# A mixture of experts on one core: seven of eight batches computed for the two picked experts only, on sorted blocks

## The reference

```python
def _mla(h, ...):      # causal attention, 16 heads of 8
    ...
def _moe(h, gate_w, w1, w2):             # 8 experts, 2 picked
    t = h.reshape(B * S, D)
    logits = t @ gate_w
    top_v, top_i = jax.lax.top_k(logits, 2)
    gates = jax.nn.softmax(top_v, axis=-1)
    combine = zeros((T, 8)).at[arange(T)[:, None], top_i].add(gates)
    hid = silu(einsum('td,edh->teh', t, w1))     # w1: 8 x 128 x 256
    ye = einsum('teh,ehd->ted', hid, w2)         # w2: 8 x 256 x 128
    return einsum('te,ted->td', combine, ye)
x = x + _mla(_rmsnorm(x, g1), ...)
x = x + _moe(_rmsnorm(x, g2), gate_w, w1, w2)
return _layernorm(x)
```

## Time and profile before

| | us |
|---|---|
| median of three runs | 658.04 (655.24 to 666.04) |
| span of the profiled execution | 658.2 |
| TensorE busy | 629.6 (96%) |
| VectorE busy | 511.7 (78%) |
| ScalarE busy | 426.6 (65%) |
| GpSimd busy | 250.2 (38%) |

### The profile page before, as it was taken

One profiled execution on the slowest core, in us unless ns is written; L12 is line 12 of the kernel. 1 busy time (PEld: TensorE's weight loads), 2 busy tenths in 40 slices (PEclk: granted clock), 3 DMA queues, 4 the chain that ended last, 5 costly groups with the idle time before them and its releaser, 6 DMA issues.

```text
span 658.2 us, 14254 instructions
## 1 busy us (share of the span) xinstructions
PE 629.6 (96%) x5056; PEld 420.7 (64%) x5056; DVE 511.7 (78%) x1871; ACT 426.6 (65%) x779; POOL 250.2 (38%) x317
## 2 busy tenths in 40 slices
PE   8999889888999999999999999999999999999996
PEld 4586545454556767676766666767676766666885
DVE  4756968958688899878888788878887888873676
ACT  4663456666667677867686768676867676756443
POOL 8130322222323365335334533353334333543442
PEclk9999968998899999999999999999999999999998
DMA  8700000000000000000000000000000000000000
GB/s 313 213 19 17 0 1 1 1 2 0 1 1 2 2 1 1 18 1 1 2 17 1 1 2 17 2 0 2 17 1 2 1 17 1 2 1 17 1 18 17
DMA packets 10072, 12.17 MB, mean 18 GB/s; under 512 B 1609, under 2 KB 8210, under 8 KB 9746
## 3 DMA queue, kind: packets, MB, share of 16 engines
q1 hardware_dynamic: 9250, 11.25, 5.2%
q10 hardware_dynamic: 752, 0.01, 0.1%
HBM read 9.16 MB, written 2.10 MB: 17 GB/s over the span
## 4 chain that ended last, share of the span: by engine, by line
PE 73%; DVE 9%; ACT 4%; issue 2%; POOL 1%; DVEq 0%; ACTq 0%; POOLq 0%
PE turn L1043 16%; PE turn L1035 14%; PE psV L1093 11%; PE psW L1081 10%; PE turn L997 6%; PE turn L987 3%; PE psS L1064 3%; DVE psS L1310 3%; PE turn L1005 2%; ACT prob L1218 1%; PE turn L1027 1%; PE turn L1016 1%; PE turn L936 1%; PE turn L928 1%; ACT X L1112 1%
## 5 line engine op out<-in xcount | busy, mean ns | idle before, releaser
L1218 ACT ACTIVATE prob<-psW 128x1024 f32<-128x1024 f32 (+1 forms) x192 | 183.1, 954 | 103.3 <-PE psW L1081 102.7
L1310 DVE CUSTOM_DVE_ANT_0 psS<-psS,maskb 128x512 f32<-128x512 f32 (+2 forms) x498 | 232.3, 518 | 19.3 <-PE psS L1064 18.4
L894 POOL TENSOR_SCALAR_AFFINE_SELECT prob<-prob 128x512 f32<-128x512 f32 x128 | 80.0, 636 | 223.4 <-ACT prob L1218 223.4
L1043 PE MATMUL turn<-wexp,late 128*128 128x128 f32 x1016 | 126.5, 278 | 0.4 <-DVE late L1370 0.4
L1043 PEld LDWEIGHTS turn<-wexp,late 128*128 128x128 f32 x1016 | 118.9, 192 | 5.7 <-issue 3.6
L1370 DVE SCALAR_TENSOR_TENSOR late<-late,turn 128x512 f32<-128x512 f32 x128 | 87.5, 685 | 37.5 <-ACT late L1180 37.0
L1180 ACT ACTIVATE late<-turn 128x512 f32<-128x512 f32 x128 | 76.3, 597 | 47.9 <-PE turn L1035 38.9
L905 POOL TENSOR_TENSOR late<-late 128x512 f32<-128x512 f32 x62 | 80.0, 1290 | 52.5 <-DVE late L1399 47.3
L1081 PE MATMUL psW<-qT,kT 26*128 26x256 f32 (+2 forms) x512 | 94.0, 404 | 4.5 <-ACT prob L1218 4.0
L1064 PE MATMUL psS<-kT,qT 24*128 24x256 f32 (+1 forms) x498 | 91.7, 405 | 2.0 <-DVE top L1310 1.7
L1093 PE MATMUL psV<-prob,va 128*32 128x512 f32 (+3 forms) x1024 | 90.7, 449 | 0.0
(11 more groups left out here) (273 smaller groups left out, 874.6 us busy)
## 6 DMA issues: line engine op xcount, KB each, us to landing
prob<-in_xT SPq DMA_DIRECT2D x4, 512.0 KB, 6.5
X<-in_x SPq DMA_DIRECT2D x1, 2048.0 KB, 15.8
out<-late SPq DMA_DIRECT2D x8, 256.0 KB, 2.3
prob<-in_wqkvT SPq DMA_DIRECT2D x1, 1024.0 KB
late<-in_w SPq DMA_DIRECT2D x1, 1024.0 KB, 10.7
prob<-in_wqkvT SPq DMA_DIRECT2D x2, 256.0 KB, 3.5
late<-in_woutT SPq DMA_DIRECT2D x1, 512.0 KB
oT<-base_rows SPq DMA_DIRECT2D x2, 256.0 KB, 3.8
```

The source lines that it names most:

```text
L894: pool.affine_select(out=blk, in_=blk, compare_op=ALU.is_ge, fill=0.0, base=0, pattern=[[0, 4], [1, P]], channel_multiplier=-1).then_inc(s ...
L1043: last = mm(into[:, D * c:D * c + D], hid[:, n % 2, k, P * c:P * c + P], wexp2[:, n, k, :], start=(k == 0), stop=(k == 1))
L1218: A(into, src, ACT.Exp).then_inc(s["exp_ready"], 1)
L1310: last = V.tensor_tensor_reduce(at, at, maskb[:, T - P * (c + 1):T], 1.0, BIG, ALU.add, ALU.max, top[:, u % 2, c, 2 * p + j:2 * p + j + 1])
```

## The change

Batch 7 (DENSE) keeps all experts for all tokens, but its up unit is one fp32 matmul of 512 columns. Batches 0 to 6 form the groups (0, 1), (2, 3), (4, 5) and (6). In a group each token has two picked experts, and each pick gets a row of a table in DRAM, sorted by expert, every expert's rows starting on a multiple of 128. The number of blocks of 128 rows is fixed at the most that can occur: 23 for two batches, 15 for one. In order of the steps:

- count and slots: TensorE counts the picks (bf16), VectorE makes from it each pick's row (index) and each block's expert (block_of), 17 small operations.
- spread: GpSimd scatters the tokens by an indirect transfer of 128 rows of 512 bytes, one for each 128 tokens and pick: 16 for two batches, 8 for batch 6, 56 in all.
- for each unit of 4 blocks, SyncE loads a block's expert number into a register and issues two transfers of 128 KB for its w1 and w2 from DRAM into a ring of 8 (weights in), then one that fetches the unit's rows, up to 256 KB (fetch). TensorE transposes them (turned), ScalarE copies them to SBUF (tokens), TensorE multiplies two blocks into a bank (pair), ScalarE takes tanh, VectorE gates, TensorE multiplies down (blocks down), ScalarE copies (save), SyncE stores (store).
- collect: GpSimd gathers each token's two results, again 56 indirect transfers; mix: VectorE adds them, weighted by gates, to the residual, which now stands in X.

The scaling of the weights (g2, 0.5) in the first layer goes, and the split of w1 too; it moves to ScalarE's copy of the tokens and into the shares. At the start of the second part SyncE clears both sorted tables, 3 MB. UNREAD_AT is not changed.

```diff
+GROUPS = [(0, 1), (2, 3), (4, 5), (6,)]
+DENSE = B - 1
+BLOCKS = [2 * n + NE - 1 for n in CHUNKS]
+UNIT = 4
+W_RING = 8
...
-UNITS = {"usual": (13, 1.0, 3), 6: (13, 1.0, 3), 7: (14.5, 1.0, 4)}
+UNITS = (14.5, 1.0, 4)
...
+BLOCKS_FROM = {0: (73.0, 1.9), 1: (121.0, 1.9), 2: (169.0, 1.0), 3: (195.0, 0.7)}
+COUNT_AT, SLOTS_AT, GATES_AT = 38.2, 38.4, 41.0
+SPREAD_FROM, SPREAD_PITCH = 38.7, 0.45
+COLLECT_AFTER, COLLECT_PITCH = 2.0, 0.45
+AFTER_COLLECT = {"mix": 1.5, "norm": 1.9, "norm root": 2.3, "result": 3.3}
...
+def group_steps(put):
+    for g, batches in enumerate(GROUPS):
+        ended = SLOTS * batches[-1]
+        begin, pitch = BLOCKS_FROM[g]
+        units = GROUP_UNITS[g]
+        put(ended + COUNT_AT, "count", g, 0)
+        put(ended + SLOTS_AT, "slots", g, 0)
+        put(ended + GATES_AT, "gates", g, 0)
+        for j in range(2 * CHUNKS[g]):
+            put(ended + SPREAD_FROM + SPREAD_PITCH * j, "spread", g, j)
+        for u in range(units):
+            load = begin - 3.0 + 0.5 * u if u < 2 else begin + pitch * (4 * u - 4.85)
+            put(load, "weights in", g, u)
+            put(load + 0.01, "fetch", g, u)
+            turn = begin - 1.0 if u == 0 else begin + pitch * (4 * u - 2)
+            put(turn, "turned", g, u)
...
+            for v in range(2):
+                at = begin + pitch * (4 * u + v)
+                put(at, "pair", g, 2 * u + v)
...
+            down = begin + pitch * (4 * u + 3)
+            put(down, "blocks down", g, u)
+            put(down + 0.6, "save", g, u)
+            put(down + 0.65, "store", g, u)
+        at = begin + pitch * (4 * units - 1) + COLLECT_AFTER
+        for b in batches:
+            for j in range(2 * C):
+                put(at + COLLECT_PITCH * j, "collect", b, j)
...
         def _(sp):
+            for what, b, n in order:
+                if what == "weights in":
+                    if n == 0:
+                        sp.wait_ge(s["owners_ready"], b + 1)
+                    q = units_before[b] + n
+                    if q >= 2:
+                        wait_full(sp, "blocks down", *unit_at[q - 2])
+                    for i in range(UNIT * n, UNIT * n + in_unit(b, n)):
...
+                        e = sp.value_load(block_of[0:1, b, i:i + 1], min_val=0, max_val=NE - 1)
+                        sp.dma_start(ring_w1(j), keep["w1_of"][ds(e, 1), :, :].rearrange("o p h -> (o p) h")
+                                     ).then_inc(ring_in[j % W_RING], 16)
+                        sp.dma_start(ring_w2(j), keep["w2_of"][ds(e, 1), :, :].rearrange("o p h -> (o p) h")
+                                     ).then_inc(ring_in[j % W_RING], 16)
+                elif what == "fetch":
+                    sp.wait_ge(s["spread_in"], 16 * moves_before[b + 1])
...
         def _(pool):
+                elif what == "spread":
...
+                    pool.indirect_dma_start(keep["sorted"][b % 2], bass.IndirectOffsetOnAxis(index[:, b, k, j:j + 1], 0),
+                                            t[:, k, :], None).then_inc(s["spread_in"], 16)
+                elif what == "collect":
...
+                        wait(pool, "mixed", b)
+                    pool.indirect_dma_start(back[:, c, j, :], None, keep["results"][g % 2],
+                                            bass.IndirectOffsetOnAxis(index[:, g, k, j:j + 1], 0)
+                                            ).then_inc(s["collected"], 16)
...
         def _(pe):
                 elif what == "hidden":
-                    for i, (w, v) in enumerate(((w1h, tTh), (w1h, tTl), (w1l, tTh))):
-                        last = mm(into[:, :], w[:, e, P * k:P * k + P], v[:, :], start=(i == 0), stop=(i == 2))
+                    mm(into[:, :], w1[:, e, P * k:P * k + P], tT[:, :], start=True,
+                       stop=True).then_inc(is_full(*step), 1)
+                elif what == "turned":
+                    q = units_before[b] + n
+                    pe.wait_ge(came_in[q % 2], 16 * (q // 2 + 1))
+                    for k in range(in_unit(b, n)):
+                        last = tr(into[:, P * k:P * k + P], came[:, q % 2, k, :], ident[:, :])
+                elif what == "pair":
...
+                    for i in range(in_pair(b, n)):
+                        j = blocks_before[b] + 2 * n + i
+                        pe.wait_ge(ring_in[j % W_RING], 32 * (j // W_RING + 1))
+                        for k in range(2):
+                            at = P * (2 * i + k)
+                            last = mm(into[:, at:at + P], ring_w1(j)[:, P * k:P * k + P],
+                                      sortedT[:, q % 2, P * (2 * v + i):P * (2 * v + i) + P], start=True, stop=True)
...
         def _(dve):
+                elif what == "mix":
+                    g = GROUP_OF[b]
+                    dve.wait_ge(s["collected"], 16 * 2 * C * (b + 1))
+                    dve.wait_ge(s["both_ready"], b + 1)
...
+                            last = V.scalar_tensor_tensor(out=X[:, C * b + c, :], in0=back[:, c, j, :],
+                                                          scalar=gates[:, g, k, j:j + 1], in1=X[:, C * b + c, :],
+                                                          op0=ALU.mult, op1=ALU.add)
```

More of the change, by code:

```diff
@@ L665 @@
 ROWS_FROM, ROWS_PITCH = -11.5, 1.5
-IN_TURN = ("rest", "apply", "half parts", "half scores", "half outputs", "half delta", "turn", "attnT", "project", "tokensT", "logits", "again", "keys", "queries", "nextT", "qkv", "hidden",
+BLOCKS_FROM = {0: (73.0, 1.9), 1: (121.0, 1.9), 2: (169.0, 1.0), 3: (195.0, 0.7)}
[3 more added lines that the diff above has]
+AFTER_COLLECT = {"mix": 1.5, "norm": 1.9, "norm root": 2.3, "result": 3.3}
+IN_TURN = ("rest", "count", "turned", "pair", "blocks down", "apply", "half parts", "half scores", "half outputs", "half delta", "turn", "attnT", "project", "tokensT", "logits", "again", "keys", "queries", "nextT", "qkv", "hidden",
            "down")
@@ L677, in expert_units @@
     return units
+def group_steps(put):
[14 more added lines that the diff above has]
+            put(turn, "turned", g, u)
+            put(turn + 0.3, "tokens", g, u)
+            for v in range(2):
+                at = begin + pitch * (4 * u + v)
+                put(at, "pair", g, 2 * u + v)
+                put(at + 0.35, "pair tanh", g, 2 * u + v)
+                put(at + 0.75, "pair gate", g, 2 * u + v)
+            down = begin + pitch * (4 * u + 3)
[6 more added lines that the diff above has]
+                put(at + COLLECT_PITCH * j, "collect", b, j)
+            at += COLLECT_PITCH * 2 * C
+            for what, later in AFTER_COLLECT.items():
+                put(at + later, what, b, 0)
+            at += AFTER_COLLECT["mix"]
 def steps_in_order():
@@ L701, in steps_in_order @@
                 put(first + WEIGHT_STEPS * g + at, what, b, g)
-        begin, pitch, lead = UNITS.get(b, UNITS["usual"])
-        for i, (what, n) in enumerate(expert_units(lead)):
+        begin, pitch, lead = UNITS
+        for i, (what, n) in enumerate(expert_units(lead) if b == DENSE else []):
             slot = first + SLOTS + begin + pitch * i
@@ L712, in steps_in_order @@
                     put(slot + pitch * IN_SLOT["unit"], "rest", b, n)
-        for (what, n), at in OF_BATCH.items():
-            own = OF_LAST if b == B - 1 else OF_SECOND if b == 1 else {}
-            put(first + own.get((what, n), at), what, b, n)
+        own = OF_LAST if b == B - 1 else OF_SECOND if b == 1 else {}
+        for (what, n), at in (OF_BATCH | own).items():
+            put(first + at, what, b, n)
         if b >= ROWS_EARLY:
@@ L823, in wait, with used_by, hid_of, t_chunks @@
                 eng.wait_ge(s[name], count)
+        units_before = [sum(GROUP_UNITS[:g]) for g in range(len(GROUPS) + 1)]
+        blocks_before = [sum(BLOCKS[:g]) for g in range(len(GROUPS) + 1)]
+        moves_before = [2 * sum(CHUNKS[:g]) for g in range(len(GROUPS) + 1)]
+        unit_at = [(g, u) for g, n in enumerate(GROUP_UNITS) for u in range(n)]
+        hidden_at = [step for step in order if step[0] in ("pair", "hidden")]
+        hidden_no = {step: i for i, step in enumerate(hidden_at)}
+        def used_by(i):
+            what, at, n = hidden_at[i]
+            return ("blocks down", at, n // 2) if what == "pair" else ("down", at, n // 2)
+        def hid_of(b, n, k):
+            return hid[:, hidden_no[("hidden", b, 2 * n + k)] % 4, :]
+        def t_chunks(b):
+            first = C * GROUPS[GROUP_OF[b]].index(b) if b in GROUP_OF else 0
+            return slice(first, first + C)
+        def in_unit(g, u):
+            return min(UNIT, BLOCKS[g] - UNIT * u)
+        def in_pair(g, v):
+            return min(2, BLOCKS[g] - 2 * v)
+        def ring_w1(j):
+            k = j % W_RING
+            return prob[:, 2, k, 0:EH] if k < 4 else ring[:, k - 4, 0:EH]
+        def ring_w2(j):
+            k = j % W_RING
+            return prob[:, 3, k, 0:EH] if k < 4 else ring[:, k - 4, EH:2 * EH]
```

(4 more changed lines are left out.)

319 lines of the change are left out of this document (243 added, 76 removed).

## The result

| | before | after |
|---|---|---|
| median | 658.96 us (655.24 to 666.04) | 792.43 us (785.58 to 796.7) |
| profiled execution, span | 658.2 us | 786.5 us |
| mean granted clock | 0.98 | 0.83 |

The ratio is 1.201, 95% interval 1.191 to 1.212: slower by a fifth, where 644 us (600 to 688) was predicted; it is taken from undisturbed runs alone, so it is not quite the quotient of the two medians. The change missed its forecast by 148 us, and in the wrong direction.

What follows compares the result with a forecast made beforehand. TensorE was taken to bound the kernel. Head 85.5, slots 0-37 99.9, 37-73 86, 73-169 226, then (57.6 + 12), tail (53.6 + 13 + 2.7) and 8 for group starts gave 644 us, range 600 to 688.

Steps and rivals of the forecast that it cites:

- counting and mixing: VectorE, slots 73 to 169: some 44 small operations for slots and gates, 11 us, and 32 mixing operations, 9.1 us.
- indirect moves: GpSimd: 56 scatters and 56 gathers at 1.04 us each, said to be covered at that price, not at 1.65.
- floor of a slot: Slots 73 to 169: three engines near 2 us plus 0.3 to 0.4 for waits, 2.35 a slot, 226 us (202 to 261).
- The block: TensorE: one transpose, two up and two down fp32 matmuls, 1.0 us a block, 84 us in all.
- Slots 37 to 73: Stage without expert work for batches 0 and 1: 2.4 us a slot, 86 us (76 to 104).
- 94 us leave TensorE: TensorE: 178 us of dense work in seven batches becomes 84 us of sorted blocks, so 94 us leave.
- C: Rival on queues: a scatter at 1.65 us or a SyncE block above 2.5 us adds 30 to 45, 680 us; chance 0.12.
- D: Rival: VectorE and ScalarE hold 2.6 us a slot, adding 24 us, 668 us; chance 0.11.
- SyncE: SyncE's queue: a register load of 0.6 us and two issues of 0.43, 1.5 us a block (0.9 to 3.1).
- Group starts: Where a group follows another, the fetch stands behind four loads: 4 us twice, 8 us in all.
- rival B: Clock falls to 0.50 in slots 37 to 73 and a third of 73 to 169: 696 us; chance 0.14.
- Batch 7 in plain fp32: Tail: an up unit as one fp32 matmul of 512 columns takes 0.87 us against 0.70, 2.7 us more.

Runs made afterwards that it cites:

- kernel with blocks only: The changed kernel without scatters, gathers and weight loads, its sorted blocks reading resident weights and zeroed rows; counting and mixing stay: 721.8 us.
- bare blocks: The changed kernel with its 84 blocks on resident weights and zeroed rows, without count, slot work, gate shares, scatters, gathers or mixes: 651.3 us; in rounds 653.3, ratio 0.990.
- attention only: The changed kernel without any sorted-expert work for batches 0 to 6; attention, norm, store and batch 7's dense experts stay: 592.4 us.
- with fillers: The changed kernel without sorted-expert work for batches 0 to 6, plus one to three unread 128x512 matmuls a slot from slot 45 to 230: 609.2 us.
- filling the whole kernel: The whole changed kernel with 227 more unread 128x512 matmuls in slots 45 to 230, one or two a slot: 812.5 us.
- placed kernel: The whole changed kernel with scatters and gathers later and further apart, and mixes and the blocks of all groups later: 763.5 us.
- count and slots only: Blocks on resident weights and zeroed rows, no moves or mixes, against the changed kernel; count, slot work, gate shares and GpSimd's slot wait kept: 689.0 us.

## Why the prediction was wrong, step by step

From slot 37 on the prediction's sum has 459 us, and the kernel took 600.7. By the table above the 142 us between them are 40 in the blocks beside the attention (30 in slots 73 to 169, 10 behind them), 60 in counting and mixing, 10 in the weight loads beyond the 33 that were priced, and 31 in the indirect moves. So three steps failed: the floor of a slot, the price of counting and mixing by busy time, and the indirect moves, which were put at nothing.

**The block: right.** 1.0 us a block on TensorE was predicted. In the kernel with blocks only the up matmuls of a pair of blocks take 0.90 us by starts at full clock (428.12 to 429.02), 0.45 a block as priced, and the bare blocks add 57 us of time for 84. Slots 37 to 73 were put at 86 us; the bare kernel has 85.7, the changed one, with its first count and scatters in them, 97.3.

**The floor of a slot: 30 us too low.** The prediction had three engines near 2 us a slot in slots 73 to 169 and added 0.3 to 0.4 for their order: 2.35, 226 us. The attention with nothing else runs at 2.28 there (218.7), so the waits between engines already made the slot, and a block is for the most part work on that chain and not in a gap: bare, 2.67 a slot, 256.3 us. The 2.1 was read from seven slots and taken for all: attention only, slots 73 to 85 do run at 2.04, but 85 to 97 at 2.46 and 109 to 121 at 2.48 (at full clock, with fillers, 2.16, 2.39 and 2.31). "94 us leave TensorE" stands and was no gain: most of the 178 us of dense matmuls had stood in slack, and all of them were worth 69 us.

**Counting and mixing: priced by busy time, about 60 us missed.** The step "some 44 small ones for slots and gates, 11 us" and "32 mixing operations, 9.1 us" put them into VectorE's sum (and 32 mixes into a stage that by the places of the change holds 16). They are chains that stand ahead of maxima on VectorE, and GpSimd, ScalarE and TensorE wait at the head of their queues for their results. This is the term that failed most. No rival held it: C had queues, but for the length of an issue, and D had VectorE's load, 24 us.

**SyncE: right in kind, size close.** 1.5 us a block, measured 1.57. (The Trainium skill, DMA: Bandwidth & Descriptors, Latency and other measured facts, has a floor of some 600 ns for the register load; by the rows 1.6 less two issues of 0.35 leaves 0.8 to 0.9, which agrees with a floor.) Group starts were put at 4 us each and the transposes waited 6.1 and 5.3; with 12 in slots 169 to 192 and 13 in the tail that is 33 us for the queue, and its waits were 36.1 (7.2 and 17.5 in those two), its worth 23 in the whole kernel. The tail has more that was not priced, since batch 6's gathers came too late as well:

```profile
754.90 2.31 DVE L1644 SCALAR_TENSOR_TENSOR X<-late,gates,X 128x128 f32<-128x128 f32 x8 [9.58 <-DMA late<-results,index]
757.13 0.68 DVE L1654 SCALAR_TENSOR_TENSOR late<-late,turn 128x512 f32<-128x512 f32 x1
```

```profile
757.86 2.08 PE L1198 MATMUL turn<-late,w 128*128 128x512 f32 x2 [10.15 <-DVE late L1654]
```

The mix of batch 6 waits 9.58 us for its gathers in VectorE's queue, the dense gate L1654 of batch 7 stands behind it, and TensorE's next up unit waits 10.15 us for that gate. The prediction took batch 7's chain alone for the tail.

**GpSimd: 1.04 us a scatter, measured 1.25 to 1.27 apart** (0.96 busy, 0.30 between). It was said to be covered at 1.04 and not at 1.65. At 0.45 slots, near 1.1 us, a burst of 16 falls behind at 1.25 already, and it starts with a wait. Price 31 us where 0 stood, 49 without the weight loads; rival C had 30 to 45.

**The clock: rival B had the sign, and its cause is not the main one.** Its clock came: in the changed kernel the main stage was at 0.80, and slots 37 to 73 took 97.3 us at 0.77. A lighter TensorE can lower the clock, as B said: with attention only slots 73 to 169 were at 0.84, with fillers at 1.00. But the bare blocks, with the sorted blocks' load on TensorE and no queue waits of the new steps, hold 0.90 and 0.96, and filling the whole kernel made it slower. So here the clock fell with the waits; that it made them dearer in turn is likely, and these runs put no size on it. (The Trainium skill, TensorE: Matmul & The Clock Gate, The HAM clock gate, has the throttled clock as the default that activity lifts; the fillers agree. By that rule slots 37 to 73 would be nearer 104 us than 76: the changed kernel's 97.3 at 0.77 are, the bare kernel's 85.7 at 0.90 are not.) How much of each added part is the wait and how much the clock behind it, these runs don't separate.

**Batch 7 in plain fp32: right.** In the tail of the changed kernel four records of L1198 take 1.72 us by starts (744.05 to 745.77) where two up units took 1.40: 0.32 an expert, 2.6 us for eight. The attention-only kernel has them in its tail too, 55.8 us against 56.0, but without the last units of batch 6 that stand there in the kernel before.

## What to carry to other kernels

Ask first what the work to be removed costs in time, not on its engine: leave it out and time the rest. Here that one run gives 69 us for 178 us of matmuls, and all that replaces them has to fit below. Then price a new step by what stands behind it in each in-order queue that it touches, its waits and the waits for its results, and not by its share of an engine that is a third idle. Loads that nobody waits for soon go behind the one small fetch that somebody waits for now.

## What the runs showed of the hardware

- An indirect DMA of 128 rows of 512 bytes occupies GpSimd 0.96 to 0.98 us, and the next starts 1.25 to 1.27 us after it.
- A register load and two transfers with that register as an offset pass SyncE in 1.57 us.
- The same instructions, slots 0 to 37, took from 93.3 us at a mean granted clock of 0.95 to 102.6 us at 0.82 in these kernels; nothing in them differs up to there, and what decides is not shown.
- Small operations of VectorE took far longer beside GpSimd's. The last one of the slot chain (1x23, to int32) takes 0.17 us at all four places of the placed kernel, at two of which a scatter of GpSimd runs beside it. In the changed kernel it took 2.12 to 2.26 us in groups 0 to 2, where GpSimd issues a scatter and behind it does a 128x512 addition, and with count and slots only, where there is the addition and no scatter, 0.75 to 0.86. In all these cases it ended within 0.05 us of the end of the addition. Two us of the 5.2 us chain above are this. First VectorE and GpSimd in the changed kernel, then in the kernel with count only:

```profile
397.37 2.12 DVE L1618 TENSOR_SCALAR block_of<-owners 1x23 int32<-1x23 f32 x1
398.17 1.28 POOL L1038 TENSOR_TENSOR X<-X,late 128x512 f32<-128x512 f32 x1
...
393.42 0.78 DVE L1591 TENSOR_SCALAR block_of<-owners 1x23 int32<-1x23 f32 x1
392.86 1.31 POOL L1017 TENSOR_TENSOR X<-X,late 128x512 f32<-128x512 f32 x1 [9.61 <-DVE index L1585]
```

What holds it until then no run here shows.
